# A mixture-of-experts stage whose rows are stored once in token order and gathered by slot lists built as one-hot products, in place of rows scattered to expert regions

## The reference

```
logits = layernorm(h) @ w_router.T          # 8 experts
top 2 of 8 experts per token, weights = softmax of the two logits
y = sum over the two experts of weight * (silu(x @ w_gate.T) * (x @ w_up.T)) @ w_down.T
out = h + layernorm(y)
```

## Time and profile before

| | |
|---|---|
| time, median of 3 runs | 1172.18 us (1171.53 to 1175.04) |
| span of the profiled execution | 1176.4 us |
| PE busy | 1024.7 us, 87% of the span |
| DVE busy | 718.6 us, 61% |
| POOL busy | 599.9 us, 51% |
| ACT busy | 578.8 us, 49% |
| share of the chain that ended last | PE 71%, DVE 9%, DMA 5%, POOL 5%, issue 4%, ACT 4% |
| mean granted TensorE clock | 0.924 of full speed |

### The profile page before, as it was taken

One profiled execution on the slowest core, in us unless ns is written; L12 is line 12 of the kernel. 1 busy time (PEld: TensorE's weight loads), 2 busy tenths in 40 slices (PEclk: granted clock), 3 DMA queues, 4 the chain that ended last, 5 costly groups with the idle time before them and its releaser, 6 DMA issues.

```text
span 1176.4 us, 19799 instructions
## 1 busy us (share of the span) xinstructions
PE 1024.7 (87%) x5646; PEld 821.8 (70%) x5647; DVE 718.6 (61%) x1864; ACT 578.8 (49%) x1273; POOL 599.9 (51%) x662
## 2 busy tenths in 40 slices
PE   5888999999999999995888972899999999999920
PEld 4678999999999999994666652466666666666610
DVE  1667999999999988995466563233333333333337
ACT  1466777877787777662658551122222222222223
POOL 4534666676667767777136557133333333333336
PEclk8999999999999999997879785899999999999965
DMA  9460001000100000111635523122222222222263
GB/s 274 118 188 10 1 13 52 1 1 5 60 1 1 24 2 10 55 54 35 215 121 173 155 58 110 32 45 45 43 46 41 45 45 45 45 45 44 41 145 123
DMA packets 54732, 75.47 MB, mean 64 GB/s; under 512 B 9348, under 2 KB 46978, under 8 KB 52612
## 3 DMA queue, kind: packets, MB, share of 16 engines
q1 hardware_dynamic: 32680, 49.24, 13.6%
q0 software_dynamic: 16640, 18.53, 9.5%
q10 hardware_dynamic: 5340, 6.83, 2.1%
HBM read 45.38 MB, written 29.14 MB: 63 GB/s over the span
## 4 chain that ended last, share of the span: by engine, by line
PE 71%; DVE 9%; DMA 5%; POOL 5%; issue 4%; ACT 4%; SPq 1%; POOLq 0%; ACTq 0%; DVEq 0%
PE bank L1495 19%; PE bank L1213 15%; PE bank L1511 9%; PE bank L1278 7%; PE bank L1273 3%; PE bank L1406 3%; PE bank L1503 2%; PE bank L1418 2%; DMA xtok<-in_tok_emb,tokens_s 2%; PE bank L1261 2%; SPq L515 1%; PE bank L1262 1%; POOL xtok L994 1%; PE bank L1486 1%; DVE arena_b L1667 1%
## 5 line engine op out<-in xcount | busy, mean ns | idle before, releaser
L1141 POOL DMA_INDIRECT yrows<-arena_b,dest_i x64 | 99.7, 1557 | 272.6 <-ACT arena_b L953 261.6
L1495 PE MATMUL bank<-arena_a,arena_b 128*128 x512 | 236.0, 604 | 0.8 <-ACT arena_b L941 0.6
L1667 DVE SCALAR_TENSOR_TENSOR arena_b<-bank,sml,arena_b 128x304 f32<-128x304 f32 (+2 forms) x384 | 195.3, 522 | 19.7 <-ACT arena_b L742 16.9
L1975 DVE TENSOR_TENSOR arena_b<-bank,arena_b 128x512 f32<-128x512 f32 x64 | 44.3, 692 | 202.3 <-PE bank L1495 202.3
L1213 PE MATMUL bank<-xt_hi,w_hi 128*128 128x308 f32 x512 | 159.7, 312 | 4.6 <-DVE arena_b L1667 3.2
L1495 PEld LDWEIGHTS bank<-arena_a,arena_b 128*128 128x128 f32 x512 | 93.1, 192 | 98.7 <-issue 95.1
L1213 PE MATMUL bank<-xt_hi,w_lo 128*128 128x308 f32 x512 | 157.1, 307 | 0.0
L1213 PE MATMUL bank<-xt_lo,w_hi 128*128 128x308 f32 x512 | 156.7, 306 | 0.0
L1032 POOL TENSOR_TENSOR u_halves<-arena_b,u_halves 128x308 fp32r<-128x308 f32 x128 | 109.6, 863 | 28.3 <-ACT arena_b L754 28.2
L1511 PE MATMUL bank<-arena_a,arena_b 128*128 x512 | 122.6, 382 | 1.1 <-DVE arena_b L1991 0.9
L1026 POOL TENSOR_TENSOR y_lo<-arena_b,y_hi 128x308 fp32r<-128x308 f32 x128 | 107.7, 855 | 26.8 <-ACT y_hi L766 26.6
(11 more groups left out here) (193 smaller groups left out, 2230.9 us busy)
## 6 DMA issues: line engine op xcount, KB each, us to landing
arena_b<-xrows SPq DMA_DIRECT2D x64, 129.5 KB, 2.1
arena_a<-in_w_gate SPq DMA_DIRECT2D x4, 1024.0 KB, 9.4
arena_a<-in_w_up SPq DMA_DIRECT2D x4, 1024.0 KB, 6.9
arena_a<-in_w_down SPq DMA_DIRECT2D x4, 1024.0 KB, 7.9
yrows<-arena_b SPq DMA_DIRECT2D x1, 3648.0 KB, 18.7
h_all<-seq SPq DMA_DIRECT2D x8, 448.0 KB
w_raw<-in_w_in SPq DMA_DIRECT2D x3, 1024.0 KB, 4.7
arena_a<-yrows SPq DMA_DIRECT2D x4, 448.0 KB
```

The source lines that it names most:

```text
L1141: pool.indirect_dma_start(yrows, bass.IndirectOffsetOnAxis(ap=dest_i[:, k:k + 1], axis=0), f_y[k], None, compute_op=ALU.add).then_inc(y_se ...
L1495: mm = pe.matmul(bank[q][:, :], x_gt[k][:, d, :], w[:, d, bass.ds(e * FFN, FFN)], start=(d == 0), stop=(d == DC - 1))
L1667: dve.scalar_tensor_tensor(acc[:, :, back_:TXT], x[:, :, 0:TXT - back_], conv_w(s // GROUPS, c, tap), acc[:, :, back_:TXT], ALU.mult, ALU. ...
L1975: dve.tensor_tensor(f_h, bank[1][:, :], f_sg, ALU.mult).then_inc(f_hh, 1)
```

## The change

Rows of a group are stored once, in token order, by plain DMAs that SP issues (`token_rows(xrows, g)`, two per group). Row 0 of `xrows` is a row of zeros. The row sets `a_x` go from four to two, and a row is 258 numbers long (the token number is gone from it). No zero rows are stored behind the experts' rows.

In the attention stage the 64 indirect sends of POOL go. For each group DVE splits a row's rank within its expert into a multiple of 128 (`slot_hi`) and a rest (`slot_lo`), and builds one-hot rows `hot_lo` (8 of 114x128, times the row's number plus 1) and `chunk`. POOL builds `hot_hi`, two products of 114x928 numbers per group (`column_hot`). PE multiplies them (`index_rows`, 8 matmuls with 232 columns) and DVE adds the result to `index_m` (`gather_index`): a table of 128 x 232 row numbers. SP's row stores stand among the weight pieces, from the eighth piece on.

Between the stages PE turns `index_m` and picks each block's column with a one-hot product; DVE copies the lists to `idx_all` (where to read) and `dest_all` (where to add; list entries of 0 go to one spare row per partition).

In the expert stage the block loads move from SP's queue to POOL's: `fetch` is an indirect DMA of 128 rows. POOL's loop is written out and not a hardware loop any more.

```diff
-            def load_block(j, k):
-                row = sp.value_load(row_i[0:1, bass.ds(j, 1)], min_val=0, max_val=XROWS - P)
-                sp.dma_start(x_g[k], xrows[bass.ds(row, P), :]).then_inc(x_in[k], 16)
...
+            def fetch(j):
+                k = j % 2
+                wait(pool, f_tr, j - 1)
+                wait(pool, f_wt, j - 1)
+                pool.indirect_dma_start(x_g[k], None, xrows, bass.IndirectOffsetOnAxis(ap=idx_all[:, j:j + 1], axis=0))\
+                    .then_inc(x_in[k], 16)
+
+            def send(j):
+                k = j % 2
                 pool.wait_ge(f_yc, j + 1)
-                pool.wait_ge(f_dest, j + 1)
-                settled(pool, pool_passed)
-                pool.indirect_dma_start(yrows, bass.IndirectOffsetOnAxis(ap=dest_i[:, k:k + 1], axis=0), f_y[k], None,
+                if j:
+                    pool.wait_ge(y_sent[1 - k], 16 * ((j + 1) // 2))
+                pool.indirect_dma_start(yrows, bass.IndirectOffsetOnAxis(ap=dest_all[:, j:j + 1], axis=0), f_y[k], None,
                                         compute_op=ALU.add).then_inc(y_sent[k], 16)
...
+            fetch(0)
+            fetch(1)
+            for j in range(BLOCKS):
+                if j + 2 < BLOCKS:
+                    fetch(j + 2)
+                send(j)
+                if j % 2:
+                    add_bias(j // 2)
...
-            def send_rows(g, first, last):
-                ...
-                for j in range(first, last):
-                    pool.indirect_dma_start(xrows, ..., a_x[g % ROW_SETS][:, b, :], None)
+            def column_hot(g):
+                pool.wait_ge(m_slot, g + 1)
+                wait(pool, m_im, g)
+                for r in range(2):
+                    hot = hot_hi[:, r * GB:(r + 1) * GB, :].rearrange("p k (e c) -> p k e c", e=EXPERTS)
+                    pool.tensor_tensor(hot, one[r]..., chunk[:, r, :, :]..., ALU.mult).then_inc(m_hi, 1)
...
+            def send_rows(g):                        # on SP
+                sp.wait_ge(m_wt, g + 1)
+                sp.wait_ge(m_row, g + 1)
+                rows = token_rows(xrows, g)
+                for cut in CUTS:
+                    sp.dma_start(rows[cut], a_x[g % ROW_SETS][cut]).then_inc(x_sent[g % ROW_SETS], 16)
             for k, (dst, src, c, cols) in enumerate(FFN_PIECES):
                 if k >= 2 and k % 2 == 0:
                     sp.wait_ge(a_h2, k)
                 sp.dma_start(dst[:, c, cols], src[:, c, cols]).then_inc(ld_ffn, 16)
+                if k > SENT_AFTER and k % 2 == 1:    # SENT_AFTER = 6
+                    send_rows((k - SENT_AFTER) // 2)
...
+            def index_rows(g):                       # on PE, between router and attended
+                pe.wait_ge(m_hi, 2 * g + 2)
+                pe.wait_ge(m_slot, g + 1)
+                for j in range(2 * GB):
+                    mm = pe.matmul(bank[6][:, 0:COLUMNS], hot_lo[:, j, :], hot_hi[:, j, :], start=(j == 0),
+                                   stop=(j == 2 * GB - 1))
...
                 if has(i - 5):
                     router(i - 5)
+                if has(i - 6):
+                    index_rows(i - 6)
                 if has(i - 4):
                     attended(i - 4, 0)
```

More of the change, by code:

```diff
@@ L373, in build @@
         slot_f = part(arena_b, 2 * GB, rows=SEQ).rearrange("p (r k) -> p r k", r=2)
+        slot_hi = part(arena_b, 2 * GB, rows=SEQ).rearrange("p (r k) -> p r k", r=2)
+        slot_lo = part(arena_b, 2 * GB, rows=SEQ).rearrange("p (r k) -> p r k", r=2)
         gap = part(arena_b, GB, rows=SEQ)
@@ L1476, in _ @@
                 .then_inc(cnt_mm, 1)
-            pe.wait_ge(tbl_ready, 2)
+            index_rows(GROUPS - 1)
+            pe.wait_ge(m_acc, GROUPS)
+            for q in range(2):
+                mm = pe.transpose(bank[0][0:HALF, q * P:(q + 1) * P], index_m[:, q * HALF:(q + 1) * HALF], ident)
+            mm.then_inc(im_turned, 1)
+            pe.wait_ge(im_copied, 1)
+            pe.wait_ge(col_picked, 2)
+            for q in range(2):
+                mm = pe.matmul(bank[1][:, 0:BLOCKS], index_t[:, q, :], pick_col[:, q, :], start=(q == 0), stop=(q == 1))
+            mm.then_inc(slots_mm, 1)
+            pe.wait_ge(tbl_ready, 1)
             pe.wait_ge(ld_ffn, 16 * len(FFN_PIECES))
@@ L1898, in place_rows, with gather_index @@
                 dve.wait_ge(m_norm, g + 1)
[L1899 to L1900 removed]
+                dve.tensor_copy(row[:, :, D + 1], idx_f[:, :, 0]).then_inc(m_row, 1)
                 chain.wait(v3_)
[L1902 removed]
+                v = chain.inc(dve.tensor_scalar(slot_hi, slot_f, 0.5 - P / 2, 1.0 / P, ALU.add, ALU.mult))
+                chain.wait(v)
+                v = chain.inc(dve.tensor_scalar(slot_hi, slot_hi, ROUND, -ROUND, ALU.add, ALU.add))
+                chain.wait(v)
+                v = chain.inc(dve.scalar_tensor_tensor(slot_lo, slot_hi, -float(P), slot_f, ALU.mult, ALU.add))
+                v = chain.inc(dve.tensor_tensor(chunk[:, :, :, :], slot_hi.unsqueeze(3).broadcast_to([SEQ, 2, GB, CHUNKS]),
+                                                number_row[0:SEQ, 0:CHUNKS].unsqueeze(1).unsqueeze(1)
+                                                .broadcast_to([SEQ, 2, GB, CHUNKS]), ALU.is_equal))
+                chain.wait(v)
+                wait(dve, m_im, g)
+                for r in range(2):
+                    for b in range(GB):
+                        batch = g * GB + b
+                        hot = dve.tensor_scalar(hot_lo[:, r * GB + b, :], number_row[0:SEQ, 0:P], slot_lo[:, r, b:b + 1],
+                                                row_no[:, batch:batch + 1], ALU.is_equal, ALU.mult)
+                hot.then_inc(m_slot, 1)
+            def gather_index(g):
+                dve.wait_ge(m_im, g + 1)
+                wait(dve, m_acc, g)
+                dve.tensor_tensor(index_m[:, :], bank[6][:, 0:COLUMNS], index_m[:, :], ALU.add).then_inc(m_acc, 1)
             text_iterations(text_step)
@@ L1927, in attn_step @@
                     routed_stats(i - 2)
+                if has(i - 4) and has(i - 3):
+                    gather_index(i - 4)
+            dve.wait_ge(numbered, NUMBERED)
             for i in range(GROUPS + LAST_LAG):
```

213 lines of the change are left out of this document (105 added, 108 removed).

## The result

The kernel after takes **1441.67 us** (median of 4 runs, 1436.54 to 1450.6) against 1173.61 us for the kernel before in runs beside it (4 runs): a ratio of 1.2304, 95% interval 1.2263 to 1.2344, slower by 268 us. The profiled execution's span is 1434.7 us (before 1176.4), its mean granted clock 0.876 (before 0.924). The traced execution of the kernel after is the fastest of its four runs (1436.54 us), while the span of the one before stands above the median of its runs, so the spans differ by 258.3 us and not by 268. The forecast was 1496 us with a range of 1380 to 1560.

The account below looks back on a forecast made before the run. PE bounds the expert stage; the fetch behind POOL's add-send would make a loop of 11.0 us a block. 1176.4 + 311 + 15 - 2 = 1500 us for the profiled execution, 1496 us for the runs, range 1380 to 1560.

Parts of the forecast that it names:

- Part 1: Expert stage: block load on POOL behind the add-send makes a loop, block 5.9 to 11.0 us, +311 us.
- C: Expert stage: fetch waits behind the add-send in the DMA rings, 1.9 us more a round, 1612 us; chance 0.08.
- D: Expert stage: fetch covered between `down` and the next `turn_block`, block stays 5.9 us, faster at 1168 us; chance 0.04.
- E: Fetch covered in the expert stage, but the changes in and after the attention stage cancel: 1172 us; chance 0.03.
- F: Expert stage: fetch half covered, landing as short as SP's 2.1 us, 61 x 1.4 = 85 us, 1270 us; chance 0.03.
- B: Expert stage: the same loop through POOL at full clock, 61 x 3.6 = 220 us, 1405 us; chance 0.20.
- A: Expert stage: the loop through POOL with the clock partly low, 1496 us, own range 1440 to 1545; chance 0.62.
- the landing: Expert stage: from the fetch's issue to its rows' landing, taken as 3.7 us, bounds 3.3 to 8.1.
- the hand-over: Expert stage: from ACT's scaled rows to the start of POOL's send, taken as 0.85 us.
- the clock: Expert stage: the stall lowers PE's clock at each `turn_block`, adding 1.5 of a possible 2.1 us a block.
- Part 2: Attention stage: PE waits for POOL's products before `index_rows`, six steps +12 us, row stores +3: +15 us (0 to +50).
- Part 3: Between the stages: last `slot_i` to first `turn_block` 16.9 us in place of 18.85, so -2 us (to +4).

Follow-up runs that it names:

- e1: Kernel after with each fetch issued one add-send earlier, ahead of the send on POOL's queue: 1196.69 us, ratio 1.0205 to the kernel before.
- e5: Kernel before with its plain block loads moved to POOL's queue behind the add-send, no lists or gathers: 1433.59 us, ratio 1.2227.
- e2b: Kernel after plus three unread matmul calls on PE ahead of each wait for the gathered rows: 1373.3 us, ratio 1.1721 to the kernel before.
- e6: Kernel after with one POOL semaphore increment put back between the send's waits and its DMA: 1478.19 us, ratio 1.2607 to the kernel before.
- e4: Kernel after with the register load for `down` issued ahead of `turn_block`'s wait on PE: 1360.6 us, ratio 1.1584 to the kernel before.
- e3: Kernel after with four row sets in place of two, two semaphores merged to make room: 1438.47 us, ratio 1.2247 to the kernel before.
- e8: Kernel after with fetch ahead of the add-send, four row sets, and `index_rows` behind `attended` on PE: 1190.33 us, ratio 1.0154 to the kernel before.

## Why the prediction was right, and where its sizes were off

**The mechanism (Part 1) was right, and shown from both sides.** e1 undoes the order and nothing else, and 245 us go; e5 gives the kernel before POOL's queue and this order, without lists or gathers, and 260 us come. Rivals C, D, E and F fell: C wanted 1.9 us on top of a fetch's landing, which took 2.8 us in all; D and E wanted a round of 5.9 us and F one of 7.3, and it was 10.0. B, the loop at full clock, fell by the clock of 0.85 in the expert stage, and e2b gives what that clock costs, 68 us. But the time of 1441.67 us lies nearer to B's 1405 than to the 1496 of A, and only 2 us inside A's own range (1440 to 1545).

**The round, term by term** (means over 60 rounds from 760 to 1370; the sum is 10.0 us, and (1376.0 - 762.7)/61 = 10.05 by the sends' starts):

| term of the sum | predicted | measured |
|---|---|---|
| `turn_block` to scaled rows, full clock | 2.6 | 2.7 |
| register load between `turn_block` and `down` | not in the sum | 0.67 |
| low clock | 1.5 | 1.2 |
| scaled rows to send | 0.85 | 0.30 |
| send to fetch | 2.2 | 2.2 |
| fetch to `turn_block` | 3.85 | 2.9 |
| sum | 11.0 | 10.0 |

The first three measured values are parts of one mean, 4.59 us from `turn_block` to scaled rows. They are parted by the kernel before, where the same stretch is 2.73 at full clock and its gap is 0.24 against 0.91. 61 rounds of 1.0 us less are 61 of the 65 us by which the forecast of 1500 lay above the span. That it came this near is in part luck: the landing, the hand-over and the clock were put 1.8 us too high together, and the register load that the sum lacked took 0.67 of that back. The bounds of the round held the landing between 3.3 and 3.7 us only, though rows gave 8.1 as its upper end, and with 3.3 their sum is 9.1 and not 9.15.

- *The landing* was the largest miss, 0.9 us. I took the row sends' 3.6 us for a gather of about the same bytes. Both ends of my range (3.3 to 8.1) lay above the median, 2.8, and "3.7" was wrong in kind: here the scatter of rows was no stand-in for the gather. The Trainium skill ("DMA: Bandwidth & Descriptors", section "Anatomy of one DMA — SWDGE (gpsimd) path") gives 2.0 us plus the bytes over 436 GB/s, an estimate of 2.3 us for this block. The trace's 2.8 us, from the issue on, lie between that and the 3.6 us that I had made of it; the 1.3 us that I had added for the making of the descriptors stands in no row.
- *The hand-over*: I wrote that I "do not credit the two waits that are gone". Not a wait but the increment in `settled` was worth the 0.55 us, by which the send now follows sooner (0.59 in e6).
- *The register load* was missing. In the kernel before, where PE does not stop, the gap is 0.24 us; behind a wait it is 0.91, and with the load ahead of the wait 0.30 (e4).
- *The clock*: the size was near (1.5 against 1.2 by the rounds, 1.1 by e2b), and the kind of loop was right, partly low. "The clock to be low when each `turn_block` starts" was wrong for the kernel after: `turn_block` took 0.44 to 0.48 us, its time at full clock, in 53 of 60 rounds, and `down` pays. In e5, with the same loop, it came about: there `turn_block` took 0.54 to 0.69 us in 49 of 59 rounds, with a granted clock of 0.54 in the 0.8 us around the one at 988.30. The Trainium skill ("TensorE: Matmul & The Clock Gate", section "HAM oscillation — how this bites in real kernels") has each round start low, in a loop whose matmuls are shorter than the DMA wait. Here they are longer (PE works 5.9 us or more and waits about 2), and 49 of 60 rounds had a slow `down` and 11 none.

**Part 2 (+15)** measured +11.0 in the two traces compared (137.1 against 126.1 us from first to last `attended`). That pair shows the change in too good a light. The same attention code took 137.1 to 142.4 us in six executions after, and 120.0 us in e5, which has the stage of the kernel before. At like granted clocks the difference is 16 to 17 us: 137.1 against 120.0 at 0.85, 142.2 (e1) against 126.1 at 0.82 and 0.80. So +15 was near; the 23 us that e1's median leaves, 2.0 of them in its expert stage, ask for no less. The parts of it were off. POOL's products took 1.76 us each, not 2.2. `index_rows` took 0.99 us at full clock, as forecast, but by the working given (0.45 us for 512 columns, eight times 232) it would be 1.6. The row stores behind two weight pieces landed 8.35 to 8.7 us after their issue, as worked out (8.5), but ACT's wait for them (L898, 17.5 us in 3 waits) was on the chain, where I let most of it hide:

```profile
631.86 8.35 DMA xrows<-arena_b
...
640.82 1.58 ACT arena_b L898 x3
642.44 1.78 PE bank L1445 x8
```

e3's chain shows that the two halves of Part 2 cover each other: take one wait away and another stands there. And that the later `weigh` on DVE stays hidden behind L884 holds only as long as the other waits are there; in e8 those 2 us are on the chain in each of six steps.

**Part 3 (-2)** measured -0.9 (38.6 against 39.5 us from the last `attended` to the first `turn_block`). The first `attended` came 2.1 us earlier than before (571.0 against 573.1), which I had not forecast; in the experiments that leave all ahead of it as it is in the kernel after it came at 570.6 to 574.4, so the traces show no shift.

## What to carry to other kernels

When a load moves to another engine's queue, ask what the instruction ahead of it waits for: here a load whose inputs were ready stood behind a send that needed the end of the work which the load was to feed, and exchanging two lines was worth 245 us. Price such a loop by its whole round, with every register load and semaphore increment in it, since what is hidden on a full engine is paid once per round in a loop that waits. Work that fills an engine's idle time by the averages (DVE at 61% here) can still lengthen each step if it stands ahead of what the next stage waits for.

## What the runs showed of the hardware beyond what I expected

- An indirect gather of 128 rows of 1,032 bytes, issued by POOL, landed 2.8 us after its issue (2.7 to 3.9), and its instruction held POOL for 0.99 us; the add-send of as many rows 3.8 and 1.59 us. A plain load of about the same size from POOL landed in 3.1 us (e5; 2.3 to 3.5), from SP in 2.1.
- A semaphore increment ahead of POOL's indirect DMA made the hand-over from ACT 0.59 us longer (e6).
- A register load of PE behind a wait showed as 0.5 us of "issue" and cost 0.61 us a round; with the load ahead of the wait `down` was slow in 24 of 62 rounds and not in 49 of 60 (e4).
- The same attention code took 137.1 us at a mean granted clock of 0.85 in the stage and 142.0 to 142.4 at 0.82 (e1, e4, e6), so one trace of each kernel does not price a change of a few us there.
- In the kernel after, the clock had in most rounds not fallen when PE resumed after its wait (1.00 from 908 to 910), but fell while `down` ran (0.63 from 910 to 912). In e5, 0.2 to 0.3 us slower a round, it was mostly down already at `turn_block` (49 of 59 rounds). In e2b 2.7 us of matmuls without use in each round kept it at 1.00 and made the kernel 68 us faster.
